# A mixture-of-experts down product: from four fp32 matmuls to twelve fp32r ones with a split w2 from DRAM, and the scaling of its result on another engine

## What is computed

```python
logits = 30.0 * jnp.tanh((x @ w_gate) / 30.0)
probs = jax.nn.softmax(logits, axis=-1)
_, idx = jax.lax.top_k(probs, 2)
mask = jax.nn.one_hot(idx, 8).sum(-2)
weights = probs * mask
for e in range(8):
    h = jax.nn.silu(x @ w1[e]) * (x @ w3[e])
    ...
```

## Time and profile before

| | before |
|---|---|
| median of 3 runs | 685.33 us (685.17 to 686.24) |
| the profiled execution | 686.1 us |
| its span, first to last instruction | 684.3 us |
| busy in the span: PE, DVE, ACT, POOL | 94%, 88%, 80%, 68% |
| TensorE's mean granted clock | 0.981 |
| DMA | 37.73 MB, mean 55 GB/s |

### The profile page before, as it was taken

The page is one execution under the profiler, slowest core; times in us unless marked ns, Lnnn a source line. Parts: engine busy times, 40 slices in busy tenths (PEclk is TensorE's granted clock), DMA queues, the critical chain, the costliest instruction groups (busy, mean ns, idle before and its releaser), DMA issues. The chain is left out here.

```text
span 684.3 us, 14974 instructions
## 1 busy us (share of the span) xinstructions
PE 641.3 (94%) x4573; PEld 588.8 (86%) x4574; DVE 599.4 (88%) x1386; ACT 550.0 (80%) x1927; POOL 466.5 (68%) x646
## 2 busy tenths in 40 slices
PE   1789999999999999999999999999998599999994
PEld 0788999999999999999999999999887588888883
DVE  7998899999999999998999999887799887777771
ACT  5898889899988998998899899988886256666660
POOL 4677786688767778777776886788665525565642
PEclk9999999999999999999999999999999589999998
DMA  7203010100020102002010110100089512333232
GB/s 228 62 2 93 2 32 1 40 25 32 2 62 1 32 2 63 32 1 64 1 32 2 55 43 2 61 3 1 1 300 399 172 39 47 47 54 54 46 46 24
DMA packets 35510, 37.73 MB, mean 55 GB/s; under 512 B 2704, under 2 KB 30352, under 8 KB 35440
## 3 DMA queue, kind: packets, MB, share of 16 engines
q1 hardware_dynamic: 31024, 30.84, 13.5%
q0 software_dynamic: 4416, 6.03, 5.5%
HBM read 31.62 MB, written 5.24 MB: 54 GB/s over the span
## 5 line engine op out<-in xcount | busy, mean ns | idle before, releaser
L1518 POOL TENSOR_SCALAR shared<-shared,rsum 128x256 f32<-128x256 f32 x256 | 143.8, 573 | 52.5 <-DVE rsum L1034 47.6
L717 ACT ACTIVATE shared<-s,nmax 128x256 f32<-128x256 f32 x256 | 122.3, 498 | 23.2 <-DVE nmax L1029 23.0
L1512 POOL TENSOR_TENSOR rstd<-rstd,half 128x7 f32<-128x7 f32 (+1 forms) x64 | 87.8, 1371 | 5.3
L1029 DVE TENSOR_REDUCE nmax<-s 128x2 f32<-128x512 f32 x128 | 86.6, 678 | 1.4 <-PE s L380 1.1
L1039 DVE TENSOR_TENSOR pt_lo<-t,pt_hi 128x512 fp32r<-128x512 f32 x124 | 84.1, 679 | 2.3 <-ACT pt_hi L725 1.3
L725 ACT CAST pt_hi<-t 128x512 fp32r<-128x512 f32 x124 | 73.9, 596 | 10.6 <-PE t L395 7.4
L733 ACT ACTIVATE shared<-route_bank,head_w 128x512 f32<-128x512 f32 (+1 forms) x124 | 81.7, 690 | 0.4 <-PE route_bank L409 0.4
L1024 DVE TENSOR_TENSOR qk_lo<-shared,qk_hi 128x512 fp32r<-128x512 f32 x96 | 77.9, 811 | 2.1 <-POOL qk_hi L1529 1.0
L380 PE MATMUL s<-qk_hi 128*128 128x256 f32 x256 | 77.3, 302 | 2.0 <-DVE qk_lo L1024 1.2
L336 PE MATMUL pj_a<-w_ring,xq 128*128 128x256 f32 x488 | 72.2, 291 | 6.3 <-POOL xq L1594 6.3
L395 PE MATMUL t<-ident,shared 128*128 128x128 f32 x496 | 75.0, 274 | 3.0 <-POOL shared L1518 1.7
(11 more groups left out here) (281 smaller groups left out, 1949.1 us busy)
## 6 DMA issues: line engine op xcount, KB each, us to landing
expert_w<-in_w SPq DMA_DIRECT2D x24, 512.0 KB, 9.3
spare<-in_wT SPq DMA_DIRECT2D x19, 256.0 KB, 3.0
wp_raw<-in_wpT SPq DMA_DIRECT2D x16, 256.0 KB, 2.9
spare<-in_wkvT SPq DMA_DIRECT2D x16, 128.0 KB, 3.3
spare<-in_wT SPq DMA_DIRECT2D x9, 128.0 KB, 3.2
spare<-in_x SPq DMA_DIRECT2D x1, 1024.0 KB, 5.9
x_hat<-acc SPq DMA_DIRECT2D x1, 1024.0 KB, 4.6
out<-spare SPq DMA_DIRECT2D x1, 1024.0 KB, 6.9
```

The source lines that it names most:

```text
L717: e = act.activation(probs[:, st, h * S:(h + 1) * S], s_bank[st][:, h * S:(h + 1) * S], ACT.Exp, bias=nmax[:, st, h:h + 1], accum_out=psum ...
L1029: dve.tensor_reduce(nmax[:, st, :], s_bank[st][:].rearrange("p (h t) -> p h t", h=2), AX, ALU.max, negate=True).then_inc(max_done, 1)
L1512: pool.tensor_tensor(rstd[:, st, c], rstd[:, st, c], half[:, c], ALU.pow).then_inc(rstd_ready, 1)
L1518: m = pool.tensor_scalar(probs[:, st, c], probs[:, st, c], rsum[:, st, h:h + 1], 1.0, ALU.mult, ALU.mult)
```

## The change

SP loads w2 of each expert during attention into `wp_raw`, POOL splits it into two parts in the free half of `wp_ring`, and SP stores the parts (1 MB for each expert) to a new DRAM tensor `w2_parts`. Only w1 and w3 are kept in `expert_w` (16 loads). For each slot SP fetches the two parts of its expert's w2 (1 MB, rows of 1 KB) into one of two buffers `w2_ring`. `hidT` gets a low part, and the down product takes twelve fp32r matmuls. The order in the steps of TensorE, ScalarE and VectorE changes, and `take_y` moves from VectorE to ScalarE.

SP, in attention, with `load_w2`, `store_w2` and the new order of the loads:

```diff
+            def load_w2(e):
+                sp.dma_start(wp_raw[:], w2[e].rearrange("(j p) h -> p j h", p=P)).then_inc(w2_loaded, 16)
+
+            def store_w2(e):
+                sp.wait_ge(w2_split, 2 * (e + 1))
+                sp.dma_start(w2_parts[e].rearrange("i j p h -> p i j h"), wp_ring[:, (e + 1) % 2].bitcast(F32))\
+                    .then_inc(route.w2_stored, 16)
+
-            for g in range(1, G):
+            for g in range(1, 3):
                 sp.wait_ge(w_ready, g)
                 load_w(g)
-                sp.wait_ge(wp_ready, g)
-                load_wp(g)
...
+            for g in range(G - 1):
+                sp.wait_ge(wp_ready, g + 1)
+                load_w2(g)
+                if 1 <= g < G - 2:
+                    sp.wait_ge(w_ready, g + 2)
+                    load_w(g + 2)
...
+                store_w2(g)
+                load_wp(g + 1)
+            sp.wait_ge(wp_ready, G)
+            load_w2(G - 1)
...
-            for e in range(E - 1):
+            for e in range(E):
                 load_expert(e)
-            sp.wait_ge(acc_read, 4 * (G - 1))
-            load_expert(E - 1, (0, 1))
-            sp.wait_ge(tile_out, ST)
-            load_expert(E - 1, (2,))
+            store_w2(G - 1)
```

```diff
@@ wp_hi
                     wait(wp_loaded, 32 * (g + 1))
+                    if g > 0:
+                        wait(route.w2_stored, 16 * g)
...
+            def w2_hi(e, a):
+                if a == 0:
+                    pool.wait_ge(w2_loaded, 16 * (e + 1))
+                    if e > 0:
+                        pool.wait_ge(out_done, 4 * e)
+                n = slice(2 * a, 2 * a + 2)
+                pool.tensor_scalar(wp_ring[:, (e + 1) % 2, 0, n], wp_raw[:, n], 1.0, 1.0, ALU.mult, ALU.mult).then_inc(w2_hi_done, 1)
+
+            def w2_lo(e, a):
+                pool.wait_ge(w2_hi_done, 2 * e + a + 1)
+                n = slice(2 * a, 2 * a + 2)
+                pool.tensor_tensor(wp_ring[:, (e + 1) % 2, 1, n], wp_raw[:, n], wp_ring[:, (e + 1) % 2, 0, n].bitcast(F32),
+                                   ALU.subtract).then_inc(w2_split, 1)
...
@@ step, b = unit's place in its group
                 scale_probs(u, 0, 1)
-                if prep and b >= 2:
-                    wp_hi(g + 1, 1 - par, b - 2)
-                    wp_lo(g + 1, 1 - par, b - 2)
+                if b == 0:
+                    wp_hi(g, par, 1)
+                    wp_lo(g, par, 1)
+                elif b < 3:
+                    w2_hi(g, b - 1)
+                    w2_lo(g, b - 1)
+                elif prep:
+                    wp_hi(g + 1, 1 - par, 0)
+                    wp_lo(g + 1, 1 - par, 0)
...
@@ the written-out end
             widen(28, 0, 1)
+            w2_hi(G - 1, 0)
+            w2_lo(G - 1, 0)
             power(31, 1)
             heads_hi(30, 2, 2)
             scale_probs(29, 1, 1)
+            w2_hi(G - 1, 1)
+            w2_lo(G - 1, 1)
             scale_probs(30, 0, 0)
```

The slots, engine by engine (SP, PE, ACT, DVE):

```diff
+            def step(n, par):
+                e = sp.value_load(slot_expert[0:1, bass.ds(n, 1)], min_val=0, max_val=E - 1)
+                if least(n, 2):
+                    sp.wait_ge(y_done, n - 1)
+                sp.dma_start(w2_ring[:, par].bitcast(F32),
+                             w2_parts[bass.ds(e, 1)].rearrange("e i j p h -> p (e i) j h")).then_inc(w2_in[par], 16)
...
             def down(n, par):
-                e = pe.value_load(slot_expert[0:1, bass.ds(n, 1)], min_val=0, max_val=E - 1)
-                pe.wait_ge(ht_ready, n + 1)
+                pe.wait_ge(ht_split, n + 1)
+                pe.wait_ge(w2_in[par], loads(n, par))
                 if least(n, 2):
                     pe.wait_ge(y_copied, n - 1)
-                for j in range(IT):
-                    m = pe.matmul(y_bank[par][:, 0:H], hidT[:, par, j * P:(j + 1) * P],
-                                  w2_sb[:, bass.ds(e, 1), j, :].rearrange("p e i -> p (e i)"), start=j == 0, stop=j == IT - 1)
+                trio = [(j, l, i) for j in range(IT) for l, i in ((hidT, 0), (hidT, 1), (hidT_lo, 0))]
+                for q, (j, l, i) in enumerate(trio):
+                    m = pe.matmul(y_bank[par][:, 0:H], l[:, par, j * P:(j + 1) * P], w2_ring[:, par, i, j],
+                                  start=q == 0, stop=q == len(trio) - 1)
                 m.then_inc(y_done, 1)
...
@@ PE step
                 more = not isinstance(n, int) or n + 1 < SLOTS
+                turn_hidden(n, par)
                 if more:
                     hidden(n + 1, 1 - par, 0)
-                turn_hidden(n, par)
-                if more:
                     hidden(n + 1, 1 - par, 1)
...
@@ ACT
+            def take_y(n, par):
+                if isinstance(n, int) and n == 0:
+                    act.wait_ge(scales_known, 1)
+                act.wait_ge(y_done, n + 1)
+                if least(n, 2):
+                    act.wait_ge(scattered, 16 * (n - 1))
+                act.activation(y_sb[:, par, :], y_bank[par][:, 0:H], ACT.Identity, scale=row_scale[:, bass.ds(n, 1)])\
+                    .then_inc(y_copied, 1)
...
                 if more:
                     rows_turned(n + 2, par)
-                    weights_high(n + 2, par, (0,))
                 act.wait_ge(ht_done, n + 1)
                 if least(n, 2):
                     act.wait_ge(y_done, n - 1)
                 act.copy(hidT[:, par, :], ht_bank[:]).then_inc(ht_ready, 1)
+                if more:
+                    weights_high(n + 2, par, (0,))
                 if not isinstance(n, int) or n + 1 < SLOTS:
                     silu(n + 1, 1 - par)
                 if more:
                     weights_high(n + 2, par, (1,))
+                take_y(n, par)
...
@@ DVE
+            def hidden_rest(n, par):
+                dve.wait_ge(ht_ready, n + 1)
+                dve.tensor_tensor(hidT_lo[:, par, :], ht_bank[:], hidT[:, par, :].bitcast(F32), ALU.subtract).then_inc(ht_split, 1)
...
                     e = expert_of(n + 2)
+                hidden_rest(n, par)
+                if more:
                     weights_rest(n + 2, par, e, 0)
...
-                take_y(n, par)
```

More of the change, by code:

```diff
@@ L305, in _, with load_expert @@
+            sp.wait_ge(wp_ready, G)
+            load_w2(G - 1)
+            def load_expert(e):
+                n = KT * w1.shape[2]
+                at = expert_w[:, 2 * e * n:2 * (e + 1) * n]
+                for i in range(2):
+                    sp.dma_start(at[:, i * n:(i + 1) * n].rearrange("p (k c) -> p k c", k=KT),
+                                 (w1, w3)[i][e].rearrange("(k p) c -> p k c", p=P)).then_inc(route.e_loaded, 16)
             sp.wait_ge(pj_done, 4 * U)
-            for e in range(E - 1):
+            for e in range(E):
@@ L1707, in _, with experts @@
             m.then_inc(route.places_set, 1)
-def experts(nc, expert_w, early, firsts, out, acc, ident, route, x_hat, SLOTS, inner):
+def experts(nc, expert_w, early, firsts, out, acc, ident, route, x_hat, SLOTS, inner, w2_parts):
     NT, H = acc.shape[1:]
@@ L1732, in bank @@
             return es.enter_context(nc.psum_tensor(name, [P, 512], F32))
-        sb("expert_home", expert_w.shape)
+        sb("expert_home", [P, E * 2 * KT * I])
+        w2_ring = sb("w2_ring", [P, 2, 2, IT, H], F32R)
+        hidT_lo = sb("hidT_lo", [P, 2, I], F32R)
+        sb("w2_gap", [P, expert_w.shape[1] - E * 2 * KT * I - 4 * IT * H - 2 * I])
         w13_hi = sb("w13_hi", [P, 2, 2, KT * I], F32R)
@@ L1785, in experts @@
         hid = sb("hid", [P, 2, I])
-        hidT = sb("hidT", [P, 2, I])
+        hidT = sb("hidT", [P, 2, I], F32R)
         y_sb = sb("y_sb", [P, 2, H])
@@ L1803, in experts @@
         scattered = sem("scattered")
+        ht_split, w2_in = sem("ht_split"), [sem("w2_in_0"), sem("w2_in_1")]
         last_known, last_ranked, fill_known, fill_found, out_known = (
@@ L1833, in _ @@
         def _(sp):
+            def step(n, par):
[4 more added lines that the diff above has]
+                             w2_parts[bass.ds(e, 1)].rearrange("e i j p h -> p (e i) j h")).then_inc(w2_in[par], 16)
+            sp.wait_ge(slots_known, 1)
+            sp.wait_ge(route.w2_stored, 16 * E)
+            steps(sp, step)
             sp.wait_ge(scattered, 16 * SLOTS)
@@ L2259, in block_kernel @@
         attention(nc, x, ctxT, wT, wkvT, wpT, cols, eye, w_gate, tables, firsts, acc, attn_gate, ident, col, half, spare, row_norm,
-                  route, x_hat, out, expert_w, early, w1, w3, w2)
-        experts(nc, expert_w, early, firsts, out, acc, ident, route, x_hat, slots, w1.shape[2])
+                  route, x_hat, out, expert_w, early, w1, w3, w2, w2_parts)
+        experts(nc, expert_w, early, firsts, out, acc, ident, route, x_hat, slots, w1.shape[2], w2_parts)
 def table_columns(experts, slots, rows):
```

39 lines of the change are left out of this document (13 added, 26 removed).

## The result

| | before | after |
|---|---|---|
| median | 685.25 us | 701.44 us |
| lowest to highest | 685.07 to 686.24 | 697.43 to 702.79 |
| profiled execution | 686.1 us | 702.79 us |
| its span | 684.3 us | 701.0 us |

The ratio is 1.0221, with a 95% interval of 1.0203 to 1.024. The change makes the kernel 16 us slower, and the time lies above the predicted range (680 to 698).

A forecast was written before the change was run, and what follows sets the result against it. TensorE's chain and the scatters' chain were taken to run nearly level, the scatters holding the end. Scatters +2.4, first scatter -0.3 and attention +1.3 gave +3.4 us, a median of 688.7 us; range 680 to 698.

The forecast's parts named there:

- What bounds, and which way it goes: Slots: TensorE's chain at 5.17 to 5.19 us and the scatters' at 4.64 run nearly level; scatters hold the end.
- The down product: TensorE, each slot: twelve products take 1.42 us in place of 1.73, 0.31 less; floor 4.88 us.
- The loop of ScalarE and VectorE: Slots: the new order closes a loop over two steps, taken at 5.0 us a slot, bounds 4.88 and 5.1.
- Attention: POOL gets 30.4 us more, costing nothing in the loop; the written-out end costs +1.3 us, bounds 0 and 3.2.
- The fetch's latency: w2 fetch per slot: needed 8.6 us after issue, lands in 7.6 with others' packets, so it has room.
- The second rival: Slots: the fetch lands late, TensorE waits at w2_in, 5.65 us a slot, +9.6, 696 us; chance 0.20.
- The scatter under the load: POOL's scatter chain beside fetches: intervals 5.2 us, between 5.02 and 5.44; chain 113.6 us against 111.2, +2.4.
- The sum: Whole kernel: scatters +2.4, first scatter -0.3, attention +1.3, together +3.4 us; median 688.7 us.
- The far bound: Scatter interval with the whole fetch ahead of it: 4.64 + 3.05 = 7.69 us.
- The third rival: Slots: scatters queue behind whole stretches of a fetch, up to 7.69 us each, +52, 737 us; chance 0.04.
- The first rows: Start of slots: 4 MB less expert loads worth nothing, since the first gather waits for VectorE's slot_token, 3.51 us.

The follow-up runs named there:

- e1: Kernel after with only the first two of 23 w2 fetches, later slots multiplying stale parts (time only): 684.90 us.
- e11: e6 with three w2 buffers and each fetch held by a bare POOL increment behind the scatter and gather three slots earlier: 733.20 us.
- e10: Kernel after with each fetch held by a bare POOL increment placed behind the gather that follows the scatter two slots earlier: 737.71 us.
- e6: Kernel after with the first fetch issued only when the rows of slots 0 and 1 have landed: 701.97 us.
- e15: e9 with the first fetch waiting for the rows of slots 0 and 1: 682.79 us.
- e9: Kernel after with w2's high parts kept in SBUF and only the low part, 512 KB, fetched per slot, whole computation: 684.88 us.
- e4: Kernel after with w2_parts laid out by partition, rows of 8 KB in place of 1 KB, same bytes: 702.61 us.
- e2: Kernel before plus an unused 1 MB fetch per slot in 1 KB rows, awaited by TensorE ahead of the down product: 693.11 us.
- e5: Kernel after with take_y moved back from ScalarE to the end of VectorE's step: 702.80 us.
- e8: Kernel after with each fetch held by a bare POOL increment placed behind the scatter two slots earlier: 730.21 us.
- e3: Kernel after fetching only w2's high part, 512 KB a slot, with the matmul count unchanged (time only): 684.76 us.
- e14: e11 with the hold given by a one-column memset behind the gather in place of the bare increment: 695.87 us.

## Why the prediction was wrong

- **What bounds, and which way it goes.** Right: the scatters' chain holds the end, and the fetches slow it. Part 4 of the page shows it; e1 shows that the fetches are the cause. It holds the end far more than before, where the chain that ended last was TensorE's for 17% of the span and the scatters' for 1%.
- **The down product.** Right: twelve products start within 603.19 to 604.48 us, 0.12 each, 1.41 in all against 1.42.
- **The loop of ScalarE and VectorE.** Nearly right and of no weight: 5.0 was taken, 4.90 measured in e1. The scaling on ScalarE takes 0.47 (0.45 taken), the low part of hidT 0.69 (0.69).
- **Attention.** Right. TensorE is busy for 99.80 us of 200 to 300 in place of 99.81, while POOL rises from 77.0 to 82.5. In the end stands the predicted gap, 1.14 us ahead of TensorE's turn at 504.89, and the first gather is 1.3 later.
- **The fetch's latency.** Right: TensorE never waits for it; it lands after 5.1 us (median), where 7.6 was allowed. The second rival is refuted. TensorE's granted clock is 1.00 over 575 to 665 us, so the clock is no cause either.
- **The scatter under the load.** This step failed. The interval was taken at 5.2, between one row of w2 at each turn (5.02) and the one late interval in the trace of before (5.44); it is 5.67. This term brought +13.4 in place of +2.4. The sum let each of a scatter's 8 rows per engine wait for one row of w2, 0.38 us in all, and took the rest from how busy the engines are. The runs show that the scatter's rows start only when the fetch is nearly through: the delay is not 0.4 us, but whatever is left of a fetch behind which a scatter lands after 5.8 us. The mean share of the engines was 94% in the forecast and 77% in the trace (88% in the first slots), and it doesn't tell the delay: e11, the kernel with the longest interval, has 59%. The far bound, 4.64 + 3.05 = 7.69, was the right mechanism: e10 reaches 7.36, from 572.03 to 704.50 us in 18 intervals. The kernel after escapes about two thirds of it since SP issues the fetch when the product ends, 0.3 to 1.5 us ahead of the scatter in most slots.
- **The third rival** named this mechanism, with its worst price, 737, and got 0.04. e10, where the fetch comes at the worst moment of those tried and TensorE waits for it too, is at 737.71. That the two agree within 1 us is luck in part: its intervals are 7.36 and not 7.69, and its first scatter starts 4.8 us later than before and not 1. The case between it and the forecast was missing: whole stretches, but with a lead.
- **The first rows.** "Four MB less of expert loads ahead of the slots are worth nothing" was said, and the two fetches that now start beside the first gathers were not costed: +2.3. The first scatter came 3.3 us later in place of the 1.0 of the sum. e6 gives 1.9 of it back at the first scatter, without a gain in the total; e15 against e9 gives 2 us.

The Trainium skill (DMA: Bandwidth & Descriptors, section Queues, rings and completion order) lets an engine leave a queue only after a whole packet of up to 64 descriptors. A fetch has 64 rows of 1 KB for each engine, so by the upper figure a scatter behind it waits for all of it. The trace agrees in effect: landings of 6.1 to 6.2 us after the fetch in e10, and no packet of POOL's queue among the first 925 of a fetch's above. The page's typical figure, 9 to 17, would free the scatter sooner, and no landing shows that. The prediction set this rule at one row a turn because a packet in the trace is one row; the page counts several descriptors to a packet, so the two packets aren't the same thing. In e4 the rows are 8 KB, 8 for each engine, and the scatters still land 5.5 to 5.8 us after the fetch (three issued 1.4 to 1.7 us ahead of the scatter, two 0.2 to 0.3 behind). No run here shows how large a packet in the page's sense was, or that this rule and no other is at work.

**What stays open.** That product, fetch and scatter move in step, with a lead near 0.9 us, is read from the times in the trace of after; no run changes the gather's place alone to test it, and the lead near 2 us in e2 has no such account. The trace gives each packet's queue and time, not its engine, so that the fetch goes ahead whole is shown for the 16 engines together, not for each. Why the engines serve the fetch first, also when it is issued 0.4 us after the scatter, is open. So is the time of 1 MB in two halves that lie evenly apart.

## What to carry to other kernels

Before putting a load beside a chain of dependent small DMAs, ask where each load falls between them. Take what is left of its time in flight, not its mean share of the engines, as the price of a meeting. Here a load of 512 KB in a step of 4.9 us fitted into the gap and cost nothing; twice that cost 0.85 us at every step. If the load can be cut by keeping a part resident, try that ahead of layouts, extra buffers or triggers: of the changes tried here that do the whole computation, it alone gave the time back (e9, 684.9).

## What the runs showed of the hardware

- A scatter of 128 rows of 1 KB that is issued up to 1.5 us after a 1 MB load, or 0.4 us before it, lands 5.7 to 6.4 us after the load's issue once one load is through before the next is issued (after from 593 us on, e5 from 616 on, e8, e10). With a load of 512 KB it lands 4.0 us after its own issue (e3), without a load after 3.8 (e1).
- While the load's packets run, those of the scatter don't start: none from 611.44 to 615.50 in after. In e1 the first starts 2.1 to 2.3 us after the scatter.
- The bytes' share of the engines doesn't tell the landing: e2 and e14, with 89% busy, land in 4.3 and 4.6 us (medians), after with 77% in 4.9, e11 with 59% in 6.6.
- A bare semaphore increment in POOL's queue ran ahead of the indirect DMAs that stand before it: in e10 it freed SP's DMA 1.5 us before the gather ahead of it was issued. A memset of one column kept its place (e14).
